# A decoder layer's feed-forward stage: floors and scales for pairs of tiles, and another order on TensorE

## The reference

```python
def _weight_quant(w):
    scale = 1.0 / jnp.clip(jnp.mean(jnp.abs(w)), 1e-05)
    wq = jnp.clip(jnp.round(w * scale), -1.0, 1.0) / scale
    return w + jax.lax.stop_gradient(wq - w)

def _act_quant(x):
    scale = 127.0 / jnp.clip(jnp.max(jnp.abs(x), axis=-1, keepdims=True), 1e-05)
    xq = jnp.clip(jnp.round(x * scale), -128.0, 127.0) / scale
    return x + jax.lax.stop_gradient(xq - x)

def _bitlinear(x, w):
    return jnp.einsum('bsi,oi->bso', _act_quant(x), _weight_quant(w))
gate = jax.nn.silu(_bitlinear(x, w_gate))
up = _bitlinear(x, w_up)
return _bitlinear(gate * up, w_down)
...
x = _layernorm(x + _L0_attn_ref(x, ...), axis=-1)
x = _layernorm(x + _L0_xattn_ref(x, ctx_1024, ...), axis=-1)
x = _layernorm(x + _L0_ffn_ref(x, L0_ffn_w_gate, L0_ffn_w_up, L0_ffn_w_down), axis=-1)
```

## Time and profile before

| | us |
|---|---|
| median of 3 runs | 713.59 (713.18 to 714.05) |
| span of the profiled execution, first to last instruction | 712.5 |
| TensorE busy | 672.1 (94%) |
| VectorE busy | 633.6 (89%) |
| ScalarE busy | 374.0 (52%) |
| GpSimd busy | 353.7 (50%) |
| steady part of the feed-forward stage (tile 4 to tile 31) | 609.36 to 699.72 |

### The profile page before, as it was taken

One profiled execution on the slowest core, in us unless ns is written; L12 is line 12 of the kernel. 1 busy time (PEld: TensorE's weight loads), 2 busy tenths in 40 slices (PEclk: granted clock), 3 DMA queues, 4 the chain that ended last, 5 costly groups with the idle time before them and its releaser, 6 DMA issues. The chain is left out here.

```text
span 712.5 us, 12566 instructions
## 1 busy us (share of the span) xinstructions
PE 672.1 (94%) x4412; PEld 491.7 (69%) x4412; DVE 633.6 (89%) x1259; ACT 374.0 (52%) x722; POOL 353.7 (50%) x491
## 2 busy tenths in 40 slices
PE   9889999999989998899999799799999999999995
PEld 3478765887747886468886586567877776666664
DVE  4998787999989999989999979748999996999997
ACT  4732157031255503463232633669777776888885
POOL 0633424646135762158451571391692224788785
PEclk9999999999999999999999999999999999999998
DMA  8630045232522436143663065730000000000012
GB/s 311 180 61 1 0 119 104 74 60 25 64 51 38 104 133 60 29 89 60 192 104 74 0 197 88 256 100 2 2 3 2 2 2 1 1 31 31 32 60 90
DMA packets 35353, 50.51 MB, mean 71 GB/s; under 512 B 4857, under 2 KB 29433, under 8 KB 35035
## 3 DMA queue, kind: packets, MB, share of 16 engines
q0 software_dynamic: 7680, 16.77, 15.1%
q1 hardware_dynamic: 26746, 32.15, 13.9%
q10 hardware_dynamic: 864, 0.79, 0.4%
HBM read 29.79 MB, written 7.34 MB: 52 GB/s over the span
## 5 line engine op out<-in xcount | busy, mean ns | idle before, releaser
L744 ACT ACTIVATE yb<-banks 128x256 f32<-128x256 f32 x64 | 24.2, 386 | 149.2 <-PE banks L445 104.1
L470 PE MATMUL banks<-xt_in,w_in 128*128 128x512 f32 x192 | 87.9, 611 | 0.2
L436 PE MATMUL banks<-inv_m,spec_y 128*128 128x256 f32 x384 | 85.5, 379 | 0.0
L390 PE MATMUL banks<-z_cplx,fwd_m 128*128 128x256 f32 x240 | 72.2, 382 | 9.7 <-DVE prod L1130 5.4
L436 PEld LDWEIGHTS banks<-inv_m,spec_y 128*128 128x128 f32 x384 | 73.0, 190 | 9.9
L391 PE MATMUL banks<-z_cplx,fwd_m 128*128 128x256 f32 x240 | 71.4, 379 | 0.0
L470 PEld LDWEIGHTS banks<-xt_in,w_in 128*128 128x128 f32 x192 | 36.7, 194 | 43.3 <-issue 39.8
L390 PEld LDWEIGHTS banks<-z_cplx,fwd_m 128*128 128x128 f32 x240 | 44.8, 190 | 19.0 <-issue 8.4
L391 PEld LDWEIGHTS banks<-z_cplx,fwd_m 128*128 128x128 f32 x240 | 45.6, 190 | 6.2
L1816 ACT ACTIVATE silu<-ps_score,gate_back 128x1024 f32<-128x1024 f32 x32 | 35.6, 1114 | 19.0 <-issue 17.5
L1786 ACT ACTIVATE prob_t<-ps_pt 128x1024 f32<-128x1024 f32 x32 | 32.7, 1022 | 24.1 <-PE ps_pt L1591 24.1
(11 more groups left out here) (299 smaller groups left out, 1726.7 us busy)
## 6 DMA issues: line engine op xcount, KB each, us to landing
x_tok<-in_x SPq DMA_DIRECT2D x8, 512.0 KB, 4.2
x_tok<-in_b_out POOLq DMA_DIRECT2D x8, 512.0 KB, 13.7
v_t<-left POOLq DMA_DIRECT2D x8, 511.5 KB, 4.5
x_t<-left POOLq DMA_DIRECT2D x8, 511.5 KB, 5.3
xt_in<-in_x_t SPq DMA_DIRECT2D x3, 1024.0 KB, 5.9
x_scratch<-x_tok SPq DMA_DIRECT2D x6, 512.0 KB, 4.0
x<-x_scratch SPq DMA_DIRECT2D x6, 512.0 KB, 9.3
out<-x SPq DMA_DIRECT2D x6, 512.0 KB, 2.9
```

The source lines that it names most:

```text
L390: mm(o, fwd_m[:, at + 2 * half + odd, :], zz[:, 0, :], start=True, stop=False)
L436: last = mm(bank[:, odd * 2 * P:(odd + 1) * 2 * P], spec_y[:, j + odd, part * D + h * P:part * D + (h + 1) * P], inv_m[:, o:o + 2 * P], st ...
L470: last = mm(proj_pair(b, t)[:, c * 512:(c + 1) * 512], w_in[:, k, TILES[t] * P:(TILES[t] + 1) * P], xt_in[:, k, c * 512:(c + 1) * 512], st ...
```

## The change

Two edits, both in the feed-forward stage.

1. VectorE's floor and reciprocal are made for two tiles at once, in the odd slot of a pair (tiles 30 and 31 apart), as one instruction on two columns each. GpSimd's factor goes with them, and `round_hidden(s)` becomes `round_hidden(s - 1)` (tile 30 is rounded in slot 30, behind tile 29).
2. On TensorE the down product of tile s-3 goes ahead of the up product of tile s+1, and the turning of tile s-2 behind it. Slots at the end are written so that down(30) stays split around the last turning, as before.

```diff
@@ TensorE, the loop over slots
-                if s - 2 == LAST:
-                    down(LAST - 1, 0, FT // 2)
-                    turn_last()
-                elif s - 2 in tiles:
-                    turn_hidden(s - 2)
+                if s == 3:
+                    pe.wait_ge(added, HALVES)
+                if s - 3 in range(LAST - 1):
+                    down(s - 3)
                 if s + 1 in tiles:
                     inner(s + 1, ps_up, w_up, h_ready, up_mm)
...
-                if s - 3 in tiles:
-                    if s == 3:
-                        pe.wait_ge(added, HALVES)
-                    down(s - 3, FT // 2 if s - 3 == LAST - 1 else 0)
+                if s - 2 == LAST:
+                    down(LAST - 1, 0, FT // 2)
+                    turn_last()
+                    down(LAST - 1, FT // 2)
+                elif s - 2 in tiles:
+                    turn_hidden(s - 2)
+                if s - 3 == LAST:
+                    down(LAST)
@@ GpSimd
-            def back_hidden(i):
-                pool.wait_ge(h_floored, i + 1)
+            def back_hidden(i, n):
+                pool.wait_ge(h_floored, i + n)
...
-                tt(down_back[:, k:k + 1], h_unit[:, k:k + 1], w_mean[:, 2:3], ALU.mult).then_inc(back_down, 1)
+                tt(down_back[:, k:k + n], h_unit[:, k:k + n], w_mean[:, 2:3].broadcast_to([P, n]), ALU.mult).then_inc(back_down, n)
...
-                back_hidden(s)
-                if s != LAST:
+                if s >= LAST - 1:
+                    back_hidden(s, 1)
+                elif s % 2:
+                    back_hidden(s - 1, 2)
+                if s != LAST and s:
+                    round_hidden(s - 1)
+                if s == LAST - 1:
                     round_hidden(s)
@@ VectorE
-                ts(h_unit[:, k:k + 1], h_peak[:, k:k + 1], CLIP, 1.0 / QMAX, ALU.max, ALU.mult).then_inc(h_floored, 1)
...
+                ts(h_unit[:, k:k + n], h_peak[:, k:k + n], CLIP, 1.0 / QMAX, ALU.max, ALU.mult).then_inc(h_floored, n)
...
-                recip(h_scale[:, k:k + 1], h_unit[:, k:k + 1]).then_inc(h_scaled, 1)
+                recip(h_scale[:, k:k + n], h_unit[:, k:k + n]).then_inc(h_scaled, n)
...
-                floor_peak(s)
-                hidden_scale(s)
+                if s % 2:
+                    floor_peaks(s - 1, 2)
+                    hidden_scales(s - 1, 2)
+                elif s == LAST - 1:
+                    floor_peaks(s, 1)
+                    hidden_scales(s, 1)
```

More of the change, by code:

```diff
@@ L1982, in round_hidden @@
                 ts(hid[:, k, :], hid[:, k, :], h_scale[:, k:k + 1], MAGIC, ALU.mult, ALU.add).then_inc(h_rounded, 1)
-            def back_hidden(i):
-                pool.wait_ge(h_floored, i + 1)
+            def back_hidden(i, n):
+                pool.wait_ge(h_floored, i + n)
                 if i >= CH:
-                    pool.wait_ge(f_added, i - CH + 1)
+                    pool.wait_ge(f_added, i - CH + n)
                 k = i % CH
-                tt(down_back[:, k:k + 1], h_unit[:, k:k + 1], w_mean[:, 2:3], ALU.mult).then_inc(back_down, 1)
+                tt(down_back[:, k:k + n], h_unit[:, k:k + n], w_mean[:, 2:3].broadcast_to([P, n]), ALU.mult).then_inc(back_down, n)
             def out_factors(n, c, k0, k1, mean_first=False):
@@ L2147, in hidden, with floor_peaks, hidden_scales @@
                     .then_inc(h_peaked, 1)
-            def floor_peak(i):
-                dve.wait_ge(h_peaked, i + 1)
+            def floor_peaks(i, n):
+                dve.wait_ge(h_peaked, i + n)
                 if i >= CH:
-                    dve.wait_ge(back_down, i - CH + 1)
+                    dve.wait_ge(back_down, i - CH + n)
                 k = i % CH
-                ts(h_unit[:, k:k + 1], h_peak[:, k:k + 1], CLIP, 1.0 / QMAX, ALU.max, ALU.mult).then_inc(h_floored, 1)
-            def hidden_scale(i):
-                dve.wait_ge(h_floored, i + 1)
+                ts(h_unit[:, k:k + n], h_peak[:, k:k + n], CLIP, 1.0 / QMAX, ALU.max, ALU.mult).then_inc(h_floored, n)
+            def hidden_scales(i, n):
+                dve.wait_ge(h_floored, i + n)
                 if i >= CH:
-                    dve.wait_ge(h_rounded, i - CH + 1)
+                    dve.wait_ge(h_rounded, i - CH + n)
                 k = i % CH
-                recip(h_scale[:, k:k + 1], h_unit[:, k:k + 1]).then_inc(h_scaled, 1)
+                recip(h_scale[:, k:k + n], h_unit[:, k:k + n]).then_inc(h_scaled, n)
             def add_down(i):
@@ L2239, in _ @@
             hidden(LAST)
-            floor_peak(LAST)
-            hidden_scale(LAST)
+            floor_peaks(LAST, 1)
+            hidden_scales(LAST, 1)
             round_last()
```

## The result

The changed kernel takes 720.47 us (median of 4 runs, 720.10 to 722.38), beside 713.73 (713.18 to 714.05) before: a ratio of 1.0101, with a 95% interval of 1.0089 to 1.0112. It is 6.7 us slower; the forecast was 720.2. The profiled execution took 720.47 us with a span of 718.7.

A forecast was written before the change was run, and what follows sets the result against it. VectorE was taken as the bound before; the change closes a loop of 3.48 us a slot, putting down(30) 6.6 us later. 712.5 + 6.6 = 719.1 of span, plus 1.1 around it, gives 720.2 us; range 718.0 to 723.5.

The forecast's parts named there:

- The bound of before and its change: Feed-forward stage: VectorE bounds at 3.347 us a slot, its list of waits empty; after the change it idles.
- The loop: TensorE and ScalarE, each slot: turning, copy, down product, up product in a closed chain of 3.48 us, whatever VectorE does.
- restart: TensorE's down product after its wait for the copy: 0.04 us more than the eight matmuls' 0.87.
- loose term: Handoff from ScalarE's copy to TensorE's down product: taken as 0.05 us; 0.15 would give 3.58 a slot.
- The end pairs: Two last slots without gate and up but with the same wait: 2.62 us each.
- Behind it: After the first half of down(30): all stands as before, the last turning not waiting for the last rounding.
- Around the span: Time outside the profiled span: 1.1 us, added to a span of 719.1.
- Waits: TensorE or its weight load waits for the copy about 0.3 us, some 28 times, 8 to 10 us in all.
- Rounding one slot later costs nothing: GpSimd's later rounding: the turning has over 2 us in hand on even tiles, so no cost.
- The clock: TensorE's clock stays at 1.00 despite a pause in every slot; the rival that it falls, 742 us, 2 in 100.
- The rival that VectorE's saving comes through: Feed-forward stage: the loop doesn't bind, VectorE's saving counts, limited by TensorE in the last slots: 709.7 us, 4 in 100.
- VectorE's load falls by 4.1: VectorE's steady slots: paired floors and reciprocals save 3.4 to 4.8 us, 4.1 in the middle.

The follow-up runs named there:

- e1: The kernel before with only TensorE's new order (down ahead of up, turning last), floors, scales and roundings single: 720.04 us, ratio 1.0082.
- e2: The changed kernel with TensorE's order as before, leaving only the paired floors and scales and the later rounding: 713.95 us, ratio 1.0000.
- e6: The changed kernel with ScalarE copying half of the turned tile once more, to scratch, ahead of the real copy: 735.75 us, ratio 1.0307.
- e3: The changed kernel with the down product moved back behind the turning, which stays behind the up product: 713.60 us, ratio 0.9993.
- e5: The changed kernel with ScalarE's copy of the hidden tile in two halves, the down product waiting for each in turn: 714.63 us, ratio 1.0010.

## Where the prediction was right, and where it wasn't

**The bound of before and its change.** Right, though the list that was read was that of the matmuls alone: TensorE's weight loads waited 3.2 us for GpSimd's input rounding between 609 and 700, in six places. VectorE, idle for 2.2 of 90.36 us, was the bound all the same; in the changed kernel VectorE waits for the up product 17 times, and its 1.9 us less of work in the window move nothing (e1 has the same window with them in).

**The loop.** Right in place and in size: 3.48 a slot forecast, 3.473 on average, and 3.48 in the slot shown. From start to start the pieces there are 0.65, 1.08, 0.88 and 0.87 us, forecast 0.64, 1.07, 0.91 and 0.86: the restart, put at 0.04, is nearer 0.01, and hundredths elsewhere make up for it. Its loose term, the handoff from the copy to the down product, was taken at 0.05 and is 0.05 in the chain (680.05 to 680.10); the other value in the rows, 0.15, belongs to a turning that waits. The slots aren't quite even: most lie between 3.31 and 3.63, and slot 9 took 4.21, with 2.86 behind it. There VectorE's gated product came late, but not so late that the up product behind it waited: TensorE's turnings stay 3.47 or 3.48 us apart through those slots too.

**The first turning** was put at 605.49 and came at 605.36; the input turning ahead of it came 0.13 us earlier than before (604.38 against 604.51). **The turning of tile 28**: 702.93 forecast, 702.68 measured. **The end pairs**: 2.62 forecast, 2.61 measured. **The first half of down(30)**: 709.88 forecast, 709.63 measured. **Behind it**: as before, forecast 9.22, measured 9.07. Together 719.1 against 718.7 of span.

**Around the span** I added 1.1 us, the median of before less its profiled span. It is 1.77 in the profiled execution of after, and near 1.8 in most runs since. The step that failed is comparing the median of several executions with the span of one: 713.59 and 712.5 were two different executions, and spans of before between 711.3 and 713.4 were seen. This miss of +0.7 and that of -0.4 in the span leave +0.3 in the time; that they partly cancel is luck. One sum was off too: a loop of 3.58 gives 723.3, not 723.0, since the handoff stands 31 times in the chain and not 28.

**Waits.** Forecast: TensorE waits for the copy some 28 times, 8 to 10 us. Its weight load waited 29 times in the loop, 11.3 us, with 1.3 more in one at the very end. From 609 to 700 it is 26 times and 8.0 us, as forecast; the rest are the waits where gate and up are missing (up to 1.3 us), and the forecast of the waits counted only the 0.3.

**Rounding one slot later costs nothing.** Right in the changed kernel, where no wait of TensorE for GpSimd is among the long ones. But the reason is that order: with the turning ahead of the up product, e2 shows 4.8 us of such waits at the weight load.

**The clock.** It stayed at 1.00 over the window, with a pause of 0.31 us in nearly every slot, and in e6 too, where TensorE was busy 89.97 of 106.94 us. The rule of the Trainium skill, TensorE: Matmul & The Clock Gate, section "A second HAM failure mode: psum-queue depth-cycling", would have had it swing; with pauses of this size it doesn't here.

**The rival that VectorE's saving comes through.** It was rightly held unlikely, but its price, 3.9 us or 709.7, was wrong. e3 takes the loop away and gains 0.3 us in the stage; in the whole its interval goes from 1.1 us faster to 0.2 slower. Two terms were missing in "VectorE's load falls by 4.1": the odd slots grow by 1.85 us up to tile 22 (floor and reciprocal on two columns take longer, with GpSimd in the way or not) while the even ones lose 2.58, and the end, taken as unchanged, loses 1.07 us there. Only the limit by TensorE in the last nine slots had been counted. Since the loop hides all this in the changed kernel, the forecast didn't depend on it.

## What to carry to other kernels

When steps of one tile are moved between slots, add up what stands on each engine between a result and its use, and compare it with the time of the engine between: a copy of 1.02 us that had a slot to itself is free, and with 1.42 us of cover for 1.73 it costs 0.31 of TensorE's time in every slot, of which 0.13 showed here, because TensorE had 0.20 to spare. A closed loop has its own period, the sum of its pieces, and no engine has to be full for it to bind; halving one piece or lengthening it by a known amount shows it. And an engine's saved work is worth at most the gap to the next bound, here 3.35 against 3.15 us a slot, and less where the saved instructions are traded for wider ones or for later results at the end.

## What the runs showed of the hardware

- A floor of 128x2 values on VectorE can end with GpSimd's instruction instead of after its own 0.17 us: four in e3 took 0.27 to 0.40 and ended 0.02 us behind it. The one on 128x1 never did: 0.14 to 0.15 in 32 of 32, and two in 0.20 or 0.21. The floor of four input columns is held too (before 0.17, 0.17 and 0.51 us, in the changed kernel 0.37, 0.17 and 0.57), but not by GpSimd's `f_rstd` at 628.12, in whose middle it took 0.17.
- The step that depends on the floor, the reciprocal, starts some 0.25 us behind the floor's start for two columns and 0.18 for one, where nothing is in the way.
- ScalarE's copy starts 0.02 to 0.03 us behind the last turning matmul's end in the chain, and the down product 0.05 behind the copy's. A turning that waits for a copy starts 0.15 behind its end (701.41 to 701.56 in the earlier trace rows).
- The time around the span is near 1.8 us in most runs, up to 2.9 in single ones of the kernel before, and 2.5 to 3.1 in six of the ten of e5.
